# The order of scores and small products in three pipelined attentions of a decoder

## The chip, the cores and the metric

One NeuronCore of one Trainium2 chip. The metric is the device time of one execution of the whole kernel in microseconds, as the median of several runs. A profiled execution gives the trace.

## What is computed

Two decoder layers on x of shape (8, 128, 128), all in float32, with a plain layer norm over `x + block(x)` after each of six blocks. Three of the blocks are attentions with 16 heads of 8 channels. They are what the change touches:

```
x = norm(x + attn(x))                # attention 1: self attention, 128 queries, 128 keys
x = norm(x + cross(x, ctx))          # attention 2: 77 keys, q and k normalised per head
x = norm(x + mixture_top2(x))
x = norm(x + topk_attention_or_ssm(x))
x = norm(x + cross(x, ctx, mask))    # attention 5: 77 keys, masked
x = norm(x + experts(x))

scores = einsum('bhqd,bhkd->bhqk', q, k) * scale
p      = softmax(scores);  o = einsum('bhqk,bhkd->bqhd', p, v);  y = o @ Wo
```

## The kernel before

All three attentions are made by one set of helpers, one for each engine: `attention_tensor` (line 1406) on TensorE, `attention_scalar` (line 633), `attention_vector` (line 945) and `attention_pool` (line 500). Each walks over a step number i, with the 8 batches (B = 8) in a software pipeline, and each engine runs its instructions in the order in which they are written. Semaphores tie the engines together. The heads stand in G = 4 groups of J = 4.

In step i TensorE does, in this order:

- `shifted(i)` (from line 1426): scores of batch i, keys on the partitions, less the row maxima (lines 1443 and 1446; in the masked attention 5 also mask products, lines 1432 and 1438), into four banks, one for each group;
- `weigh(i-1)` (line 1462): probabilities times values;
- `flips(i)` (from line 1468): the output projection of batch i-3 (line 1473), the transpose of the maxima of batch i+1 (line 1477) and of the normalised output of batch i-2 (line 1480), into one bank;
- `scores(i+2)` (line 1422, with mask products at line 1418 in attention 5): scores of the batch two steps on, queries on the partitions, for the maxima alone;
- the transposes of outT of batch i-1 (line 1508).

ScalarE does exponentials (i,0) and (i,1) (line 641), copies outT of batch i-1 (line 652), copies the flipped bank (line 657), then does exponentials (i,2) and (i,3).

VectorE does the residual add of batch i-3 (line 974), which reads the flipped bank and waits for ScalarE's copy of it; the maximum of group 0 of batch i+2 (line 952); the reciprocal of batch i-1 (line 983), which waits for the outT transposes; the maximum of group 1; the normalisation into oN (line 995); the maxima of groups 2 and 3; a first remainder (line 962); the layer norm's apply for batch i-4 (line 1004), which waits for rstd from GpSimd; the second remainder; and the statistics of batch i-3 (lines 1010 to 1012). In attention 5 one more small instruction (line 987) follows the reciprocal. In attention 1 other small work stands behind steps 1, 2 and 3: the head sums for the keys of attention 2 and weight preparation.

GpSimd raises the variance to the power -1/2 for each batch (line 504). In attention 1 it first does three long powers (line 534) that need the head sums of VectorE's step 1, and two more between the batches.

PSUM has eight banks. Seven form a ring. The list `BURSTS` says in which order slots of the ring are given out: in each step four for the exponentials, one for the flips, four for the maxima. A slot waits for the reader of the slot seven places before it (`wait_bank`, line 149 on). For a slot of the flips the reader is ScalarE's copy and, from the third step on, VectorE's residual add.

Of the kernel before, what the change touches and what calls it, by code (L numbers as in the profile page):

```python
# [23 lines left out]
ALU = mybir.AluOpType  # L24
# [3 lines left out]
B, T, D = 8, 128, 128  # L28
# [71 lines left out]
RING_BANKS = [0, 1, 2, 3, 4, 5, 7]  # L100
BURSTS = [("max", 0), ("flip", -1), ("max", 1)]
for _i in range(B):
    BURSTS += [("exp", _i), ("flip", _i)] + ([("max", _i + 2)] if _i + 2 < B else [])
SLOTS = [(what, i, g) for what, i in BURSTS for g in range(1 if what == "flip" else G)]
PLACE = {slot: n for n, slot in enumerate(SLOTS)}

# [75 lines left out]
def _build(nc, ctx, a, out):  # L182
    def sb(name, shape, dt=F32):
        return ctx.enter_context(nc.sbuf_tensor(name, shape, dt))
# [4 lines left out]
    PS = ctx.enter_context(nc.psum_tensor("PS", [128, 8, 512], F32))  # L189
# [70 lines left out]
    R = sb("R", [128, B, D]); st = sb("st", [128, B, 6]); mv = sb("mv", [128, B, 2]); ve = sb("ve", [128, B]); rstd = sb("rstd", [128, B])  # L260
# [621 lines left out]
    def _(dve):  # L882
        V_ = nc.vector

        def step(ins):

            dve.wait_ge(dve_step.sem, dve_step.then(ins))
# [57 lines left out]
        def attention_vector(at, between):  # L945
            nk = at.nk

            def maximum(b, g):
                dve.wait_ge(at.scores_ready, G * b + g + 1)
                if b >= 3:  # L950
                    dve.wait_ge(at.flipped_ready, b - 2)
                V_.tensor_reduce(mxp[:, b % 3, g, 0:J],  # L952
                                 PS[:, at.bank("max", b, g), 0:J * nk].rearrange("p (j k) -> p j k", j=J),
                                 axis=AX.X, op=ALU.max).then_inc(at.max_ready, 1)

            def remainder(b, k):
                if k == 0:
                    dve.wait_ge(at.max_ready, G * (b + 1))
                else:
                    dve.wait_ge(at.part_ready, 2 * b + 1)  # L960
                whole = mxp[:, b % 3, :, J * k:J * (k + 1)]
                V_.tensor_tensor(mxp[:, b % 3, :, J * (k + 1):J * (k + 2)], whole, upper(mxp)[:, b % 3, :, J * k:J * (k + 1)],
                                 ALU.subtract).then_inc(at.part_ready, 1)

            for i in range(-2, B + 4):
                ahead, done, added, left = i + 2 < B, 0 <= i - 1 < B, 0 <= i - 3 < B, 0 <= i - 4 < B
                b, n, r = i - 4, i - 1, i - 3
                if added:
                    dve.wait_ge(at.proj_ready, r + 1)
                    if i < B + 2:  # L970
                        dve.wait_ge(at.flipped_copied, i + 2)
                    if r == 0 and not at.masked:
                        dve.wait_ge(at.xb_ready, 1)
                    V_.tensor_tensor(R[:, r, :], at.XB[:, r, :], PS[:, at.bank("flip", i), 2 * T:3 * T], ALU.add)\
                        .then_inc(at.residual_ready, 1)
                if ahead:
                    maximum(i + 2, 0)
                if done:
                    o = PS[:, at.out_bank(n), :].rearrange("p (h w) -> p h w", h=H)
                    dve.wait_ge(at.out_ready, n + 1)  # L980
                    if n >= 2:
                        dve.wait_ge(at.normed, n - 1)
                    ins = V_.reciprocal(rs[:, n % 2, :].rearrange("p (h o) -> p h o", o=1), o[:, :, HD:HD + 1])
                    if at.masked:

                        step(ins)
                        ins = V_.tensor_scalar(rs[:, n % 2, :], rs[:, n % 2, :], anykey[:], None, ALU.mult)
                    inverted = dve_step.then(ins)
                if ahead:
                    maximum(i + 2, 1)  # L990
                if done:
                    dve.wait_ge(dve_step.sem, inverted)
                    if n >= 2:
                        dve.wait_ge(at.flipped_ready, n + 2)
                    V_.tensor_tensor(oN[:, n % 2, :].rearrange("p (h d) -> p h d", h=H), o[:, :, 0:HD],
                                     rs[:, n % 2, :].rearrange("p (h o) -> p h o", o=1).to_broadcast([128, H, HD]),
                                     ALU.mult).then_inc(at.normed, 1)
                if ahead:
                    maximum(i + 2, 2)
                    maximum(i + 2, 3)  # L1000
                    remainder(i + 2, 0)
                if left:
                    dve.wait_ge(at.rstd_ready, b + 1)
                    V_.tensor_scalar(at.Xout[:, b, :], R[:, b, :], mv[:, b, 0:1], rstd[:, b:b + 1],
                                     ALU.subtract, ALU.mult).then_inc(at.x_ready, 1)
                if ahead:
                    remainder(i + 2, 1)
                if added:
                    dve.wait_ge(at.residual_ready, r + 1)
                    step(V_.bn_stats(st[:, r, :], R[:, r, :]))  # L1010
                    step(V_.bn_aggr(mv[:, r, :], st[:, r, :]))
                    V_.tensor_scalar(ve[:, r:r + 1], mv[:, r, 1:2], EPS, None, ALU.add).then_inc(at.eps_ready, 1)  # L1012
                if i in between:
                    between[i]()
# [22 lines left out]
        for c in range(2):  # L1037
            i = take(f"v1.{c}")
# [56 lines left out]
        i = take("logits8")  # L1095
# [60 lines left out]
        i = take("k5.1")  # L1156
# [12 lines left out]
        i = take("rank")  # L1169
# [3 lines left out]
        i = take("cumU")  # L1173
# [127 lines left out]
        for c in range(2):  # L1301
            i = take(f"dl.{c}")
# [11 lines left out]
        for e in range(E1 + 1):  # L1314
            if e < E1:
                for k in range(NI * 2):
                    n = e * NI * 2 + k
                    c, i = k // NI, k % NI
# [7 lines left out]
            if e == 0:  # L1326
                i = take("logits6")
# [28 lines left out]
    def _(pe):  # L1356
# [49 lines left out]
        def attention_tensor(at, between, idle, opening):  # L1406
# [5 lines left out]
            def scores(b):  # L1412

                for g in range(G):
                    at.wait_bank(pe, "max", b, g)
                if at.masked:
                    for g in range(G):
                        M_(PS[:, at.bank("max", b, g), 0:J * nk].rearrange("p (j k) -> p j k", j=J), identb[:],
                           maskneg[:].rearrange("p (o k) -> p o k", o=1).to_broadcast([128, J, nk]), start=True, stop=False)
                for g in range(G):  # L1420
                    dst = PS[:, at.bank("max", b, g), 0:J * nk].rearrange("p (j k) -> p j k", j=J)
                    M_(dst, qT[rows(g), b, :], at.kM[rows(g), :, b, :], start=not at.masked, stop=True)\  # L1422
                        .then_inc(at.scores_ready, 1)
# [27 lines left out]
            def weigh(b):  # L1451

                if b == 0:
                    aring.drain(pe)
                if b == B - 1:
                    at.wait_flip_read(pe, B - 2)
                elif b:
                    pe.wait_ge(at.normed, b)
                for g in range(G):
                    pe.wait_ge(at.exp_ready, G * b + g + 1)  # L1460
                    for j in range(J):
                        ins = M_(PS[32 * j:32 * j + 32, at.out_bank(b), 128 * g:128 * g + 128], at.V[0:nk, b, J * g + j, :],  # L1462
                                 PT[0:nk, b % 2, g, j, :], start=True, stop=True)
                ins.then_inc(at.pv_done, 1)
# [29 lines left out]
            for i in range(B + 4):  # L1494
                if i < B:
                    shifted(i)
                if i == 0:
                    opening[4]()
                if 0 <= i - 1 < B:
                    weigh(i - 1)  # L1500
                if i < B + 3:
                    flips(i)
                if i + 2 < B:
                    scores(i + 2)
                if 0 <= i - 1 < B:
                    pe.wait_ge(at.outT_copied, i)
                    for g in range(G):
                        ins = nc.tensor.transpose(PS[:, at.out_bank(i - 1), 128 * g:128 * g + 128], outT[:, g, :], ident[:])  # L1508
                    ins.then_inc(at.out_ready, 1)
                if i in between:  # L1510

                    pe.wait_ge(at.exp_ready, G * B)
                    between[i]()
# [158 lines left out]
        i = fill(dring, "scol")  # L1672
# [6 lines left out]
        i = fill(dring, "rank")  # L1679
# [5 lines left out]
        i = fill(dring, "cumU")  # L1685
# [53 lines left out]
        for e in range(2):  # L1739
            if e:  # L1740
                pe.wait_ge(event("sa_ready"), 1)
            for n in range(2):
                for c in range(4):
                    for a in range(2):
                        g = 2 * e + a
                        r = slice(32 * g, 32 * g + 32)
# [124 lines left out]
        for c in range(2):  # L1871
            i = fill(dring, f"dposA.{c}")
# [5 lines left out]
        for c in range(2):  # L1878
            if c:
                pe.wait_ge(event("chosen_copied"), 7 + NH)  # L1880
            i = fill(dring, f"dposS.{c}")
# [7 lines left out]
        for c in range(2):  # L1889
            dring.wait_copied(pe, f"dposS.{c}")  # L1890
            i = fill(dring, f"dl.{c}")
# [90 lines left out]
```

## Time and profile before

| | |
|---|---|
| median of 3 runs | 433.56 us (433.10 to 434.45) |
| the profiled execution | 434.33 us, of it span 432.5 us |
| TensorE matmul busy | 391.3 us (90%) |
| TensorE weight load busy | 262.1 us (61%) |
| VectorE busy | 280.9 us (65%) |
| ScalarE busy | 235.6 us (54%) |
| GpSimd busy | 130.5 us (30%) |
| attention 1, first to last shifted product | about 22.8 to 64 us |
| attention 2, the same | about 91.9 to 123 us |
| attention 5, the same | about 292 to 330 us |

Busy time overlaps between engines. The matmul's share is that of a pipelined engine, so 90% is not 90% of its peak. The chain of waits follows the work that ended last backwards; it names for each piece of time the engine that was waited for. The timeline gives the instructions in order of time.

### The profile page before, as it was taken

How to read it: one execution, taken by the hardware profiler on the slowest of the kernel's cores; microseconds unless marked ns; L12 is line 12 of the kernel's file. 1: busy time of each engine (PE TensorE's matmuls, PEld its weight loads, DVE VectorE, ACT ScalarE, POOL GpSimd, SP SyncE). 2: the span in 40 equal slices, each digit the busy share in tenths (PEclk: the TensorE clock that was granted, in tenths of full speed). 3: DMA queues.
4: the chain of work that ended last, by engine and by line, in shares of the span. 5: the costliest groups of instructions: out<-in, count | busy, mean ns of one | idle time of the engine just before them, and what ended most of it. 6: DMA issues, size and time to landing. Idle time of an engine off the chain costs nothing.

```text
span 432.5 us, 10063 instructions
## 1 busy us (share of the span) xinstructions
PE 391.3 (90%) x4041; PEld 262.1 (61%) x4050; DVE 280.9 (65%) x705; ACT 235.6 (54%) x441; POOL 130.5 (30%) x120
## 2 busy tenths in 40 slices
PE   5989798889999999977999999898999899999992
PEld 2556566546675946555676767645777466666662
DVE  6769656754765586897799897732566544444446
ACT  1855444736668267799999993025555442222220
POOL 6936952300113050004889893100011100000001
PEclk9999979999999999999999999989999999999998
DMA  6320000000000000020223220450000000000001
GB/s 176 74 49 2 4 2 2 1 2 3 3 5 0 2 0 2 6 109 23 90 89 102 93 81 2 131 163 2 3 4 4 2 0 0 2 0 1 2 0 48
DMA packets 16881, 13.84 MB, mean 32 GB/s; under 512 B 6548, under 2 KB 14133, under 8 KB 16837
## 3 DMA queue, kind: packets, MB, share of 16 engines
q1 hardware_dynamic: 15538, 12.51, 10.0%
q10 hardware_dynamic: 1299, 0.71, 0.5%
q8 instruction: 32, 0.52, 0.5%
q14 instruction: 12, 0.10, 0.1%
HBM read 12.64 MB, written 0.57 MB: 31 GB/s over the span
## 4 chain that ended last, share of the span: by engine, by line
PE 69%; ACT 11%; DVE 10%; POOL 5%; issue 4%; POOLq 0%; DVEq 0%; ACTq 0%
PE PS L1830 9%; PE PS L1909 6%; PE PS L1913 6%; PE PS L1940 6%; PE PS L1385 5%; PE PS L1443 5%; PE PS L1817 4%; POOL hr L534 4%; ACT att L641 3%; PE PS L1422 3%; PE PS L1371 2%; PE PS L1391 2%; PE PS L1508 2%; PE PS L1462 2%; ACT outT L652 2%
## 5 line engine op out<-in xcount | busy, mean ns | idle before, releaser
L641 ACT ACTIVATE att<-PS 77x512 f32<-77x512 f32 (+1 forms) x96 | 51.7, 591 | 47.2 <-PE PS L1446 47.2
L952 DVE TENSOR_REDUCE mxp<-PS 128x4 f32<-128x308 f32 (+1 forms) x96 | 48.0, 536 | 34.3 <-PE PS L1422 34.3
L878 ACT ACTIVATE kM<-PS 128x512 f32<-128x512 f32 x32 | 19.1, 597 | 55.5 <-PE PS L1909 54.4
L504 POOL TENSOR_TENSOR rstd<-ve,neg_half 128x1 f32<-128x1 f32 x24 | 13.1, 547 | 114.6 <-DVE ve L1012 114.6
L1258 DVE TENSOR_TENSOR_SCAN big<-big,PS 128x768 f32<-128x768 f32 x22 | 38.1, 1743 | 3.4 <-PE PS L1817 3.3
L1324 DVE TENSOR_TENSOR big<-kM,PS 128x512 f32<-128x512 f32 x32 | 21.9, 687 | 27.3 <-PE PS L1913 26.0
L498 POOL TENSOR_TENSOR rstd<-ve,neg_half 128x4 f32<-128x4 f32 x6 | 6.2, 1029 | 102.2 <-DVE ve L908 102.2
L1909 PE MATMUL PS<-xT,V 128*128 128x512 f32 x64 | 33.0, 597 | 1.1 <-DVE xT L1312 0.8
L1913 PE MATMUL PS<-xT,V 128*128 128x512 f32 x64 | 32.7, 592 | 0.0
L1940 PEld LDWEIGHTS PS<-big 128*128 128x128 f32 x256 | 29.7, 192 | 3.3 <-issue 3.3
L1371 PE MATMUL PS<-negsel,identb 128*128 128x512 bf16 x101 | 26.1, 400 | 6.1 <-DVE negsel L1024 4.4
L1940 PE MATMUL PS<-big 128*128 128x128 f32 x256 | 29.7, 275 | 0.0
L1446 PE MATMUL PS<-flipped,negsel 32*77 32x128 bf16 (+1 forms) x384 | 24.8, 219 | 0.0
L831 ACT ACTIVATE att<-big,BT 128x256 f32<-128x256 f32 x58 | 24.6, 497 | 0.0
L534 POOL TENSOR_TENSOR hr<-hvar,half_bh 77x32 f32<-77x32 f32 (+1 forms) x5 | 22.0, 4419 | 7.0 <-DVE hvar L935 7.0
L1345 DVE SCALAR_TENSOR_TENSOR R<-PS,aff,R 128x128 f32<-128x128 f32 x56 | 15.8, 345 | 11.2 <-PE PS L1940 11.2
L1443 PE MATMUL PS<-qT,kM 32*77 32x128 f32 x512 | 20.8, 276 | 1.8 <-ACT att L641 1.1
L1371 PEld LDWEIGHTS PS<-negsel,identb 128*128 128x128 bf16 x109 | 10.4, 102 | 19.1 <-issue 4.9
L1913 PEld LDWEIGHTS PS<-xT,V 128*128 128x128 f32 x64 | 12.2, 190 | 15.3 <-issue 14.8
L657 ACT ACTIVATE flipped<-PS 128x128 f32<-128x128 f32 (+1 forms) x33 | 10.7, 325 | 18.2 <-PE PS L1477 10.0
L1817 PE MATMUL PS<-ident,att 128*128 128x128 f32 x128 | 19.3, 273 | 1.2 <-ACT att L831 1.2
L1258 DVE TENSOR_TENSOR_SCAN untransposed<-untransposed,PS 128x768 f32<-128x768 f32 x10 | 17.5, 1748 | 4.4 <-PE PS L1817 4.1
(368 smaller groups left out, 894.6 us busy)
## 6 DMA issues: line engine op xcount, KB each, us to landing
kM<-Cdram SPq DMA_DIRECT2D x6, 384.0 KB, 3.5
XH<-Cdram SPq DMA_DIRECT2D x5, 384.0 KB, 3.3
xT<-Cdram SPq DMA_DIRECT2D x5, 384.0 KB, 3.4
V<-in_L_ffn_Wg SPq DMA_DIRECT2D x1, 1024.0 KB, 5.4
V<-in_L_ffn_Wu SPq DMA_DIRECT2D x1, 1024.0 KB, 8.0
out_x<-X SPq DMA_DIRECT2D x2, 256.0 KB, 2.3
ctxN<-in_ctx ACTq DMA_DIRECT2D x1, 308.0 KB
X<-in_x ACTq DMA_DIRECT2D x1, 256.0 KB, 4.0
```

The source lines that it names most:

```text
L534: P_.tensor_tensor(out=hr1[0:NC, n], in0=hvar[0:NC, n], in1=half_bh[0:NC, 0:n.stop - n.start], op=ALU.pow)\
L641: A_(PT[0:nk, i % 2, g], bank4(at.bank("exp", i, g), nk), ACT.Exp, scale=at.scale)\
L952: V_.tensor_reduce(mxp[:, b % 3, g, 0:J], PS[:, at.bank("max", b, g), 0:J * nk].rearrange("p (j k) -> p j k", j=J), axis=AX.X, op=ALU.max) ...
L1258: V_.tensor_tensor_scan(hst[m % NHS], dA[m % NDA], dBu[m % NDB], 0.0, ALU.mult, ALU.add)\
L1371: M_(PS[:, bank, :], identb[:], negsel[:].rearrange("p j t -> p (j t)"), start=True, stop=True)
L1443: M_(PS[0:nk, at.bank("exp", b, g), j * T:(j + 1) * T], at.kM[rows(g), j, b, :], qT[rows(g), b, :], start=not at.masked, stop=False)
L1446: ins = M_(PS[0:nk, at.bank("exp", b, g), j * T:(j + 1) * T], negsel[rows(g), j, 0:nk], upper(flipped)[rows(g), (b - 1) % 2, 0:T], start=F ...
L1817: ins = nc.tensor.transpose(dBu[n % NDB][:, 128 * k:128 * (k + 1)], scaled[s % 2][k][:, 128 * h:128 * (h + 1)], ident[:])
L1830: ins = M_(y_piece(h, lo, hi), ident[:], hC[n % NHC][:, lo:hi], start=False, stop=(n // NH == DS - 1 and (h, lo) != (0, 512)))
L1909: M_(PS[:, n % 2, :], Wg6[:, e, i * 128:(i + 1) * 128], half(xT, c), start=True, stop=True)\
L1913: M_(PS[:, 2 + n % 2, :], Wu6[:, e, i * 128:(i + 1) * 128], half(xT, c), start=True, stop=True)\
L1940: ins = M_(PS[:, 4 + (2 * e + c) % 4, b4 * D:(b4 + 1) * D], hidE[e % 2][:, i, b * T:(b + 1) * T], Wd6[:, NI * e + i, :], start=(i == 0), s ...
```

## The change

Three orders change, and no instruction is added or removed. In `BURSTS` the slots of the maxima of batch i+2 come ahead of the slot of the flips. On TensorE `scores(i+2)` is issued ahead of `flips(i)`. On VectorE the residual add moves from the head of the step to behind the normalisation, between the maxima of groups 1 and 2. ScalarE's and GpSimd's orders stay as they are.

```diff
 for _i in range(B):
-    BURSTS += [("exp", _i), ("flip", _i)] + ([("max", _i + 2)] if _i + 2 < B else [])
+    BURSTS += [("exp", _i)] + ([("max", _i + 2)] if _i + 2 < B else []) + [("flip", _i)]
@@ attention_vector
                 b, n, r = i - 4, i - 1, i - 3
-                if added:
-                    dve.wait_ge(at.proj_ready, r + 1)
-                    if i < B + 2:
-                        dve.wait_ge(at.flipped_copied, i + 2)
-                    if r == 0 and not at.masked:
-                        dve.wait_ge(at.xb_ready, 1)
-                    V_.tensor_tensor(R[:, r, :], at.XB[:, r, :], PS[:, at.bank("flip", i), 2 * T:3 * T], ALU.add)\
-                        .then_inc(at.residual_ready, 1)
                 if ahead:
                     maximum(i + 2, 0)
@@ behind the normalisation into oN
+                if added:
+                    dve.wait_ge(at.proj_ready, r + 1)
+                    if i < B + 2:
+                        dve.wait_ge(at.flipped_copied, i + 2)
+                    if r == 0 and not at.masked:
+                        dve.wait_ge(at.xb_ready, 1)
+                    V_.tensor_tensor(R[:, r, :], at.XB[:, r, :], PS[:, at.bank("flip", i), 2 * T:3 * T], ALU.add)\
+                        .then_inc(at.residual_ready, 1)
                 if ahead:
                     maximum(i + 2, 2)
                     maximum(i + 2, 3)
@@ attention_tensor
                 if 0 <= i - 1 < B:
                     weigh(i - 1)
+                if i + 2 < B:
+                    scores(i + 2)
                 if i < B + 3:
                     flips(i)
-                if i + 2 < B:
-                    scores(i + 2)
                 if 0 <= i - 1 < B:
                     pe.wait_ge(at.outT_copied, i)
```

## Rows read from the trace of the kernel before

**Rows 1.** The page, part 4: shares of the chain that ended last.

```profile
PE 69%; ACT 11%; DVE 10%; POOL 5%; issue 4%; POOLq 0%; DVEq 0%; ACTq 0%
```

**Rows 2.** Timeline, attention 2, step 4: start, us, engine, line, what; at last steps 5, 7.

```profile
113.76 0.46 PE L1443 MATMUL PS<-qT,kM 32*77 32x128 f32 x8 [0.16 <-ACT att L641]
...
115.21 1.07 ACT L641 ACTIVATE att<-PS 77x512 f32<-77x512 f32 x2 [1.55 <-PE PS L1446]
...
116.72 0.80 PE L1422 MATMUL PS<-kM,qT 32*128 32x308 f32 x8
...
117.10 1.07 ACT L641 ACTIVATE att<-PS 77x512 f32<-77x512 f32 x2
117.31 0.29 DVE L974 TENSOR_TENSOR R<-XB,PS 128x128 f32<-128x128 f32 x1 [0.96 <-ACT flipped L657]
...
117.45 0.66 PE L1508 MATMUL PS<-ident,outT 128*128 128x128 f32 x4
...
118.14 0.26 DVE L983 RECIPROCAL rs<-PS 128x16 f32<-128x16 f32 x1
...
118.27 0.46 PE L1443 MATMUL PS<-qT,kM 32*77 32x128 f32 x8 [0.16 <-ACT att L641]
118.32 0.42 DVE L952 TENSOR_REDUCE mxp<-PS 128x4 f32<-128x308 f32 x1
...
121.96 0.46 PE L1443 MATMUL PS<-qT,kM 32*77 32x128 f32 x8
```

**Rows 3.** Timeline, attention 2: exponentials of step 0, maximum 1 of step 1.

```profile
94.61 1.07 ACT L641 ACTIVATE att<-PS 77x512 f32<-77x512 f32 x2
...
96.08 0.46 PE L1443 MATMUL PS<-qT,kM 32*77 32x128 f32 x8 [0.72 <-DVE mxp L952]
...
100.29 0.41 DVE L952 TENSOR_REDUCE mxp<-PS 128x4 f32<-128x308 f32 x1
...
100.36 0.46 PE L1443 MATMUL PS<-qT,kM 32*77 32x128 f32 x8 [0.28 <-ACT att L641]
```

**Rows 4.** Timeline, attention 5: start of shifted and maximum 1, steps 2 and 6.

```profile
302.40 0.41 PE L1432 MATMUL PS<-first,maskrep 32*77 32x512 bf16 x4 [0.17 <-issue]
...
302.70 0.47 DVE L952 TENSOR_REDUCE mxp<-PS 128x4 f32<-128x308 f32 x1
...
323.87 0.41 PE L1432 MATMUL PS<-first,maskrep 32*77 32x512 bf16 x4 [0.16 <-issue]
...
324.18 0.47 DVE L952 TENSOR_REDUCE mxp<-PS 128x4 f32<-128x308 f32 x1
```

**Rows 5.** Timeline, attention 1: starts of steps 4 and 5, with the maxima between.

```profile
42.87 0.50 PE L1443 MATMUL PS<-qT,big 32*128 32x128 f32 x8 [0.37 <-DVE mxp L952]
...
47.17 0.69 DVE L952 TENSOR_REDUCE mxp<-PS 128x4 f32<-128x512 f32 x1
...
47.95 0.63 DVE L952 TENSOR_REDUCE mxp<-PS 128x4 f32<-128x512 f32 x1
...
48.11 0.50 PE L1443 MATMUL PS<-qT,big 32*128 32x128 f32 x8 [0.38 <-DVE mxp L952]
```

**Rows 6.** Timeline, attention 1: GpSimd's powers, and what comes behind them.

```profile
36.36 16.22 POOL L534 TENSOR_TENSOR hr<-hvar,half_bh 77x32 f32<-77x32 f32 x3 [7.04 <-DVE hvar L935]
...
53.13 0.35 DVE L1004 TENSOR_SCALAR X<-R,mv,rstd 128x128 f32<-128x128 f32 x1 [2.96 <-POOL rstd L504]
...
53.62 0.47 PE L1477 MATMUL PS<-ident,mxp 128*128 128x128 f32 x1 [2.52 <-DVE mxp L962]
...
54.23 2.09 PE L1422 MATMUL PS<-big,qT 32*128 32x512 f32 x8
...
62.45 0.50 PE L1443 MATMUL PS<-qT,big 32*128 32x128 f32 x8
```

**Rows 7.** Windows of attention 1: stretch, length, busy by engine, granted clock, DMA.

```profile
16.80:27.70 10.90, 9.18 (x91) 4.72 (x91) 8.07 (x15) 7.33 (x19) 7.23 (x9) 1.00 0.43 87
...
53.00:58.00 5.00, 4.38 (x26) 2.18 (x30) 2.54 (x9) 1.36 (x3) 5.00 (x4) 0.52 0.00 0
```

## Prediction

> **What bounds the kernel now.** I read the chain of waits first: TensorE has 69% of it, ScalarE 11%, VectorE 10% [rows 1]. The change touches only the three attentions, so I went to the timeline there, step by step. Call S the start of a step, the first product of shifted(i). In attention 2, TensorE runs shifted, weigh, flips, scores and the four outT transposes with hardly a gap: S is 113.76, the last transpose ends at 117.45+0.66 = 118.11, and the next S is 118.27 [rows 2]. Before that S TensorE stood still for only 0.16 us. ScalarE's second exponential pair ended at 117.10+1.07 = 118.17, so that pair and TensorE's own order bind almost together. In attention 5 the mask products make the step longer and TensorE binds alone: it stands for 0.16 us with the cause "issue" [rows 4]. In attention 1 the maximum of the first group binds: it ends at 47.17+0.69 = 47.86, the next S comes 0.25 us later at 48.11, and the row names VectorE's mxp as what ended the gap [rows 5]. So I take 0.25 us from the end of a maximum to the product that waits for it, and 0.10 us from the end of an exponential (118.17 to 118.27).
>
> Attention 1 also holds one large stall. GpSimd's three long powers (line 534) run from 36.36 to 52.58, and only behind them does it give rstd of the first batch. VectorE stands 2.96 us for it, until 53.13, at line 1004; the second remainder comes behind that, and flips(5) on TensorE waits 2.52 us until 53.62 [rows 6]. Through the stretch 53 to 58 the granted clock is 0.52, that is mostly the 1.2 GHz level, where 16.8 to 27.7 has 1.00 with TensorE busy for 9.18 of 10.90 us [rows 7].
>
> **The change part by part.** No instruction is added or removed. Three orders change.
>
> *TensorE.* scores(i+2) moves ahead of flips(i). The sum of the work is a permutation, so the outT transposes end at the same distance from S as now, 4.35 us in attention 2. flips(i) ends later by the length of the scores: 117.45-116.72 = 0.73 us in attention 2 [rows 2]. ScalarE's order is not changed: outT copy, flipped copy (line 657), then exponentials 2 and 3. The flipped copy waits for flips(i), and behind it in ScalarE's queue stand the two exponentials whose slots shifted(i+1) takes. So exp(i,3) ends 0.73 later, 118.90, and S could come at 119.00 instead of 118.27: +0.73.
>
> *Slots.* With nine slots a step and seven banks, shifted(i+1) now waits for exp(i,2), exp(i,3), flip(i) and max(i+2,0). After the change it is exp(i,2), exp(i,3), max(i+2,0) and max(i+2,1). That is a wait for one more maximum. On VectorE the reciprocal stands between maxima 0 and 1 and waits for the outT transposes, which stay last in TensorE's step. In the trace the reciprocal starts at 118.14, 0.03 after the last transpose, and maximum 1 runs from 118.32 to 118.74 [rows 2]. None of this moves in relation to S, so the next S can't be before 118.74+0.25 = 118.99: +0.72. The two ways give the same, and I take this one, since it gives every step from two rows: end of maximum 1, plus 0.25, less the next S. scores(i+3) in turn waits for maxima 2 and 3, for the read of flip(i) with its residual, and for exp(i+1,0). The last of these ends at about 115.21+0.54 = 115.75 (half of the pair's 1.07). The moved scores start a flips length before 116.72, so this is covered as long as the few products of flips take under 0.9 us, and they take some 0.6. flips(i) itself waits for exp(i,1), ended at 116.28, and now starts a flips length before 117.45: covered too.
>
> *VectorE.* The residual add (line 974) goes behind the normalisation, so maximum 0 no longer stands behind it. What waited for maximum 0 now waits for maximum 1 as well, so this buys nothing at the S. It delays maxima 2 and 3 by its own 0.29 us [rows 2]; they are wanted only at the next scores. I take zero, with that cover; without it 0.3 us a step.
>
> *Attention 2.* Five steps end in an S behind a scores. The first: 100.29+0.41+0.25-100.36 = 0.59; the last 0.72 [rows 2, 3]. The second is like the first (0.57), the third and fourth like the last (0.71, 0.72): together 3.3. Step 0 has no outT; there the exponential pair ends at 94.61+1.07, plus 0.73 and 0.10 gives 96.51 against S = 96.08: +0.4 [rows 3]. Sum **+3.7**, bounds 2.2 (each of the five shorter by the 0.25 of the hand-over, and step 0 by half) and 5.2 (each longer by the 0.3 of the residual add).
>
> *Attention 5.* The maximum is preceded by one more small instruction. First step: 302.70+0.47+0.25-302.40 = 1.02; last: 324.18+0.47+0.25-323.87 = 1.03 [rows 4]. The three between are 1.03, 1.04 and 0.93: together 5.05. Step 0 as in attention 2, +0.4. Sum **+5.5**, bounds by the same rule 4.0 and 7.0.
>
> *Attention 1.* Same rule: 47.95+0.63+0.25-48.11 = 0.72 a step [rows 5], four steps 2.9 with the others at 0.75, 0.71 and 0.72; step 0 is worth 0.3 by the exponential way. So S(5), now 48.11, comes at 51.3. GpSimd's powers start off VectorE's step 1, whose maxima move by some 0.2 us only, so rstd comes at about 53.3. By then maxima 2 and 3 and the first remainder of batch 6 have ended (about 52.9), VectorE waits 0.4 instead of 2.96, and the second remainder is there at 53.8, before flips(5) wants it: that now stands behind shifted, weigh and scores, which in attention 2 take 117.45-113.76 = 3.69 less the flips, so it comes at 54.1 or later. **The stall is filled by the slower steps and the clock has no long gap to fall in.** Step 5 is as long as step 4, 48.11-42.87 = 5.24 [rows 5], plus 0.72: S(6) = 57.3. Step 6 has no scores; attention 2 needs 121.96-118.27 = 3.69 for it [rows 2], and with the wider keys here I take 3.8: S(7) = 61.1 against 62.45 now [rows 6]. Sum **-1.4**, bounds -2.6 and +0.1 (five steps of the same 0.25 and 0.3). What is late next is maximum 1 in every step.
>
> Total -1.4+3.7+5.5 = **+7.8 us**. The profiled execution took 434.33 us (span 432.5); that would become 442.1. It lies 0.77 above the median of the runs shown, 433.56, so by the median **441.4 us**. Everything behind an attention only shifts: no transfer lands late there.
>
> **The clock, and the rule of the Trainium skill on it.** After the change TensorE stands about 0.9 us a step in attention 2 (119.00 less 118.11) and 1.2 in attention 5. The trace has a fall after a gap of 2.52 us [rows 6, 7] and none in a stretch that is 84% busy. The Trainium skill (TensorE: Matmul & The Clock Gate, The HAM clock gate) says that the clock follows how busy TensorE has recently been and that the unthrottled state has to be earned by activity. By that rule the added gaps could bring a fall of their own, which would add the price of the rival below; a step that stands 0.9 of 5.2 us is 83% busy, near to the stretch that kept its clock, so I forecast none.
>
> **The rivals.**
> 1. *The clock falls in the longer gaps.* The fall in attention 1 cost, from S(5) to S(7), 62.45-48.11 = 14.34 us against 5.24+3.8 = 9.0: 5.3, of which 2.5 are the stall and 2.8 the lower clock. One fall anywhere gives 444.2, one in each attention 449.8. Chance 0.12.
> 2. *The stall in attention 1 stays,* because the powers start later with the steps: then attention 1 costs +3.9 instead of -1.4: 446.7. Against it: VectorE's step 1 hardly moves. Chance 0.06.
> 3. *The slot wait bites only half.* If maximum 1 gets through earlier than its row shows, or the exponentials are released sooner, half of 9.2 in attentions 2 and 5 is left: about 437. Chance 0.14.
> 4. *Faster.* Place: flips(5) of attention 1. scores(7) now stands behind the 2.5 us stall and runs at the low clock, 2.09 us [rows 6]. Ahead of flips it runs while TensorE waits. If the steps did not get longer, this alone would give 433.56-2.0 = 431.5. It decides from a step price under 0.2 us (2.0 over ten steps of attentions 2 and 5). Against it: two independent ways both give 0.7 or more. Chance 0.07.
> 5. *The order does nothing,* since TensorE is full either way: 433.6. Chance 0.03.
>
> The forecast itself has 0.58. The range 437.0 to 446.0 takes in rival 3's value, the one fall of rival 1 and the bounds of the three sums (2.2+4.0-2.6 = 3.6 above the median gives 437.2, 5.2+7.0+0.1 = 12.3 gives 445.9). A measurement of this kernel can tell about 0.3% from no change. Slower by more than that 0.89, within 0.04, faster 0.07.
>
> **What would show it.** In the profile after: in attention 2, S to S of 5.2 instead of 4.5; in attention 5 of 6.4 to 6.5 instead of 5.4 to 5.5; a TensorE gap of about 1 us ahead of line 1443 or 1432 put down to VectorE's mxp or ScalarE's att; the reciprocal still right behind the transposes. In attention 1 steps of 5.9, VectorE's wait at line 1004 under 1 us, no granted clock under 0.9. The prediction is wrong if the exponentials 2 and 3 start before the flipped copy, if the reciprocal finds its transposes done earlier, or if the clock falls.

## The result, and the profile after

The changed kernel takes 440.53 us (median of 4 runs, 439.86 to 442.34) against 433.33 us before (431.92 to 434.45): a ratio of 1.017, 95% interval 1.013 to 1.022. That is slower by 7.2 us, clear of no change (the interval is +5.7 to +9.5 us); 441.4 was forecast, +7.8. All ratios below are to runs of the kernel before from the same round, and leave out the few that were over 1.5% slower than the fastest of their kernel.

The page of the changed kernel, parts 1 and 4 (busy time by engine, and the shares of the chain that ended last). GpSimd has gone from 5% to 1% of the chain, ScalarE from 11% to 12%, TensorE from 69% to 72% [rows 1]:

```profile
span 439.1 us, 10057 instructions
PE 385.6 (88%) x4041; PEld 260.4 (59%) x4050; DVE 281.1 (64%) x705; ACT 236.5 (54%) x441; POOL 130.6 (30%) x120
PE 72%; ACT 12%; DVE 10%; issue 4%; DMA 1%; POOL 1%; POOLq 0%; DVEq 0%; ACTq 0%
```

TensorE is busy for less time than before (385.6 against 391.3 us) in a longer span: the added time is gaps. The busy time itself is shorter because the granted clock was higher in the profiled execution, 0.990 on average against 0.980.

Timeline of the changed kernel, attention 2, one whole step from S = 110.14 to S = 115.39 (start, us, engine, line, what):

```profile
110.14 0.46 PE L1443 MATMUL PS<-qT,kM 32*77 32x128 f32 x8 [1.05 <-ACT att L641]
...
111.45 1.08 PE L1462 MATMUL PS<-att,V 77*32 77x128 f32 x32
112.46 0.80 PE L1422 MATMUL PS<-kM,qT 32*128 32x308 f32 x8
113.19 0.49 PE L1473 MATMUL PS<-Wp,flipped 128*128 128x128 f32 x2
...
113.74 0.60 PE L1508 MATMUL PS<-ident,outT 128*128 128x128 f32 x4
113.94 0.38 ACT L657 ACTIVATE flipped<-PS 128x256 f32<-128x256 f32 x1 [0.74 <-PE PS L1480]
114.22 1.07 ACT L641 ACTIVATE att<-PS 77x512 f32<-77x512 f32 x2
114.38 0.26 DVE L975 RECIPROCAL rs<-PS 128x16 f32<-128x16 f32 x1 [0.62 <-PE PS L1508]
114.55 0.42 DVE L952 TENSOR_REDUCE mxp<-PS 128x4 f32<-128x308 f32 x1
...
115.39 0.46 PE L1443 MATMUL PS<-qT,kM 32*77 32x128 f32 x8 [1.05 <-ACT att L641]
```

ScalarE now waits 0.74 us for the flips before it can copy them; before, the timeline shows no wait there. The exponentials behind the copy end at 115.29, and S comes 0.10 later. The reciprocal still starts right behind the transposes (114.34), and maximum 1 ends at 114.97. The gap of TensorE ahead of S is 1.05 us, where it was 0.16 [rows 2].

The span by stages, from the two timelines (S(0) is the first shifted product of an attention, S(7) the last batch's):

| stretch | before | after | change |
|---|---|---|---|
| start to S(0) of attention 1 | 22.86 | 23.22 | +0.36 |
| attention 1, S(0) to S(7) | 39.59 | 37.55 | -2.04 |
| to S(0) of attention 2 | 29.50 | 29.69 | +0.19 |
| attention 2, S(0) to S(7) | 30.01 | 33.86 | +3.85 |
| to S(0) of attention 5 | 170.13 | 169.08 | -1.05 |
| attention 5, S(0) to S(7) | 35.82 | 40.93 | +5.11 |
| the rest | 104.59 | 104.77 | +0.18 |
| span | 432.5 | 439.1 | +6.6 |

In attention 1, GpSimd's rstd still comes late, and VectorE still waits at line 1004, but for 1.19 us instead of 2.96, and TensorE no longer waits for what lies behind it. Timeline and windows of attention 1 after; the window answers to the second line of [rows 7]:

```profile
53.59 1.14 PE L1422 MATMUL PS<-big,qT 32*128 32x512 f32 x8
53.82 0.35 DVE L1004 TENSOR_SCALAR X<-R,mv,rstd 128x128 f32<-128x128 f32 x1 [1.19 <-POOL rstd L504]
54.08 0.17 DVE L962 TENSOR_TENSOR mxp<-mxp 128x16 f32<-128x16 f32 x1
...
54.98 0.27 PE L1477 MATMUL PS<-ident,mxp 128*128 128x128 f32 x1
...
60.77 0.50 PE L1443 MATMUL PS<-qT,big 32*128 32x128 f32 x8
```

```profile
53.00:58.00 5.00, 3.91 (x81) 2.74 (x73) 3.74 (x12) 2.68 (x6) 5.00 (x5) 1.00 0.01 3
```

The transpose of the maxima, which stood 2.52 us for the second remainder before [rows 6], runs at once, scores(7) take 1.14 us instead of 2.09, and the granted clock is 1.00 where it was 0.52.

### The profile page after: what moved, and what is told of

Same layout as the page of the kernel before. It is cut to its first block, busy times and chain, and to the rows that moved or that the text cites. A ratio compares the mean times of both kernels' runs of the same rounds, so it can differ in the third digit from the quotient of the medians.

```text
span 439.1 us, 10057 instructions
## 1 busy us (share of the span) xinstructions
PE 385.6 (88%) x4041; PEld 260.4 (59%) x4050; DVE 281.1 (64%) x705; ACT 236.5 (54%) x441; POOL 130.6 (30%) x120
## 4 chain that ended last, share of the span: by engine, by line
PE 72%; ACT 12%; DVE 10%; issue 4%; DMA 1%; POOL 1%; POOLq 0%; DVEq 0%; ACTq 0%
PE PS L1830 9%; PE PS L1443 6%; PE PS L1940 6%; PE PS L1909 6%; PE PS L1913 6%; PE PS L1385 5%; ACT att L641 5%; PE PS L1422 5%; PE PS L1462 4%; PE PS L1817 4%; PE PS L1371 3%; PE PS L1391 2%; PE PS L1642 2%; PE PS L1508 2%; PE PS L1380 1%
## 5 line engine op out<-in xcount | busy, mean ns | idle before, releaser
L1913 PEld LDWEIGHTS PS<-xT,V 128*128 128x128 f32 x64 | 12.2, 190 | 15.3 <-issue 14.8
L1443 PEld LDWEIGHTS PS<-qT,kM 32*77 32x77 f32 x512 | 15.9, 143 | 8.3 <-ACT att L641 7.7
```

The costliest lines, as they stand in the source:

```text
L1443: M_(PS[0:nk, at.bank("exp", b, g), j * T:(j + 1) * T], at.kM[rows(g), j, b, :], qT[rows(g), b, :], start=not at.masked, stop=False)
L1913: M_(PS[:, 2 + n % 2, :], Wu6[:, e, i * 128:(i + 1) * 128], half(xT, c), start=True, stop=True)\
```

## The experiments

**Theory:** two ways of nearly the same length make a step longer: ScalarE's queue (scores, flips, flipped copy, exponentials 2 and 3, S) and VectorE's (outT transposes, reciprocal, maximum 1, S). Each alone gives about 0.7 us a step. **Rivals:** only one of the two counts. The three parts of the change were tried alone on the old kernel, and the change was tried without its VectorE part; then each way was cut in the changed kernel. The step times below are from S to S in the profiled execution of each run. A step with a projection is one of the steps 3 to 5, in which flips also makes the output projection and VectorE does a residual add.

**The slots alone** (on the kernel before):

```diff
-    BURSTS += [("exp", _i), ("flip", _i)] + ([("max", _i + 2)] if _i + 2 < B else [])
+    BURSTS += [("exp", _i)] + ([("max", _i + 2)] if _i + 2 < B else []) + [("flip", _i)]
```

> The kernel before, with the new order of slots alone; TensorE and VectorE keep their old order. Theory (two ways of equal length, through VectorE's maximum 1 and through ScalarE's queue): shifted(i+1) now waits for maximum 1, which stands behind the reciprocal and the outT transposes, so the steps grow although TensorE's order is the old one: attention 2 step 4 to about 5.23 us (4.51 before), attention 5 to 6.4 (5.4 before), attention 1 to 5.96 (5.24), the cause of the gap named as VectorE's mxp; total about 441. Rival (ScalarE's queue alone makes the change slower, the slot wait is covered): steps stay 4.5 and 5.4, total 433.3.

Measured: 446.47 us, ratio 1.029 (1.022 to 1.036). The slot wait alone costs more than the whole change. Its timeline in attention 2:

```profile
113.08 0.46 PE L1443 MATMUL PS<-qT,kM 32*77 32x128 f32 x8 [0.88 <-DVE mxp L952]
...
115.66 0.49 PE L1473 MATMUL PS<-Wp,flipped 128*128 128x128 f32 x2 [0.19 <-ACT att L641]
...
117.89 0.41 DVE L952 TENSOR_REDUCE mxp<-PS 128x4 f32<-128x308 f32 x1
...
118.57 0.46 PE L1443 MATMUL PS<-qT,kM 32*77 32x128 f32 x8 [0.89 <-DVE mxp L952]
```

S is 0.27 after the end of maximum 1, as the theory has it, and the step is 5.49 us, not 5.23. The 0.26 more is the second row: with flips still ahead of scores on TensorE, the slot of flips(i) now waits for exponential (i,1). In the changed kernel scores stand there instead, and cover that wait: flips start at 113.19, 0.5 us after the exponential ended (111.59+1.08 = 112.67). The other attentions have the same addition (6.70 in attention 5, 6.22 in attention 1), which is why the total is 5 us above the 441 expected. The rival (steps stay) has fallen.

**TensorE's order alone** (on the kernel before, `scores(i + 2)` ahead of `flips(i)`, slots and VectorE as they were):

```diff
+                if i + 2 < B:
+                    scores(i + 2)
                 if i < B + 3:
                     flips(i)
-                if i + 2 < B:
-                    scores(i + 2)
```

> The kernel before, with scores ahead of flips on TensorE alone; slots and VectorE as before. Theory (two equal ways): the exponentials 2 and 3 stand behind the flipped copy, which now comes 0.7 us later: attention 2 step 4 about 5.2 us, attention 5 about 6.2 with a projection and 6.0 without, attention 1 about 5.9; total about 440.5. Rival (the slot wait alone makes the change slower): steps stay 4.5 and 5.4, total 433.3.

Measured: 446.83 us, ratio 1.031 (1.023 to 1.038); steps with a projection take 5.59 in attention 2 and 6.57 to 6.67 in attention 5. Timeline of its attention 2:

```profile
118.64 0.80 PE L1422 MATMUL PS<-kM,qT 32*128 32x308 f32 x8 [0.28 <-ACT att L641]
...
121.56 0.46 PE L1443 MATMUL PS<-qT,kM 32*77 32x128 f32 x8 [1.05 <-ACT att L641]
```

ScalarE's exponentials release S in attention 2, as expected (in steps 3 to 5 of attention 1 the rows name mxp). Again about 0.35 is on top, and again it is a slot that doesn't match: in the old order the last slot of scores waits for exponential (i,1), and the first row has that wait. Neither addition was expected; both totals came out 5 to 6 us above their expectation. So each half alone is dearer than the whole (+12.7 and +13.3 us, the ratio less one times 433.3, against +7.2 for the whole).

**VectorE's order alone** (on the kernel before, the residual add behind the normalisation as in the change, nothing else):

> The kernel before, with the residual add behind the normalisation on VectorE alone; slots and TensorE as before. In the old slot order shifted(i+1) waits for the read of flip(i), and from step 3 on that is the residual add, now behind the reciprocal and the normalisation. Theory (an order pays only with the slots that match it): in attention 2 steps 1 and 2 stay at 4.3 to 4.4 us, steps 3 to 5 grow from 4.51 to about 5.6 with VectorE's R as the cause; attention 5 steps 3 to 5 to about 6.7; in attention 1 about half of the stall is filled; total about 440. Rival (the place of this add costs nothing wherever it stands, as the prediction had it for the changed kernel): 433.3.

Measured: 441.01 us, ratio 1.018 (1.011 to 1.024). Steps 1 and 2 of attention 2 stay at 4.28 and 4.40, steps 3 to 5 are 5.72 (6.93 in attention 5), and the releaser is the residual add:

```profile
117.33 0.46 PE L1443 MATMUL PS<-qT,kM 32*77 32x128 f32 x8 [1.37 <-DVE R L996]
```

The part alone costs +7.6 us by the same rule, no more and no less than the whole within the intervals.

**The change without VectorE's part** (the residual add back at the head of the step):

> The changed kernel, with the residual add back at the head of VectorE's step; slots and TensorE as changed. Prediction's term: the move is worth nothing, since maximum 1 waits for the reciprocal anyway: steps stay at 5.23 (attention 2) and 6.39 (attention 5), total 440.5. Rival (with scores ahead of flips the add at the head makes maximum 0 wait for the flipped copy, and maximum 1 behind it): steps with a projection grow to about 5.75 in attention 2, 7.0 in attention 5 and 6.6 in attention 1, total about 446.

Measured: 448.81 us, ratio 1.035 (1.029 to 1.042). Here the prediction's term falls and the rival holds: steps with a projection are 5.70 (attention 2), 7.02 (attention 5) and 6.65 or more (attention 1), the others as in the changed kernel. Timeline of attention 2:

```profile
120.19 0.29 DVE L974 TENSOR_TENSOR R<-XB,PS 128x128 f32<-128x128 f32 x1 [2.54 <-ACT flipped L657]
120.39 0.47 DVE L952 TENSOR_REDUCE mxp<-PS 128x4 f32<-128x308 f32 x1
120.78 0.25 DVE L983 RECIPROCAL rs<-PS 128x16 f32<-128x16 f32 x1
120.94 0.41 DVE L952 TENSOR_REDUCE mxp<-PS 128x4 f32<-128x308 f32 x1
...
121.61 0.46 PE L1443 MATMUL PS<-qT,kM 32*77 32x128 f32 x8 [1.51 <-DVE mxp L952]
```

The add waits for the flipped copy, now late, and holds up maximum 0; the reciprocal starts 0.7 us after the transposes and no longer right behind them.

One step of attention 1 took 8.24 us, 1.5 more than the steps on both sides of it. TensorE had stood for 2.01 us before it, and the granted clock fell. Behind the next gap, of 1.96 us, it stayed at 1.00 (51 to 58), and behind the third, of 1.93, it fell again (0.60 from 60 to 64). In the same execution the gaps of 1.51 us a step in attention 2 and of 1.83 in attention 5 had a granted clock of 1.00. Window of attention 1:

```profile
48.00:52.00 4.00, 4.00 (x48) 2.55 (x40) 1.16 (x7) 1.64 (x4) 4.00 (x1) 0.68 0.01 2
```

So the rival of the prediction in which longer gaps bring the clock down did come true in this variant, though not in the changed kernel.

**ScalarE's way cut** (on the changed kernel, exponentials ahead of the flipped copy):

```diff
+                if 0 <= i < B:
+                    exponentials(i, (2, 3))
                 if i < B + 2:
                     ...
                     A_(flipped[:, i % 2, lo:hi], PS[:, at.bank("flip", i), lo:hi], ACT.Copy).then_inc(at.flipped_copied, 1)
-                if 0 <= i < B:
-                    exponentials(i, (2, 3))
```

> The changed kernel, with ScalarE's exponentials 2 and 3 ahead of its flipped copy. Theory (two equal ways): the way through maximum 1 is still there, so nothing is gained: attention 2 step 4 stays within 0.1 of 5.23 us, attention 5 within 0.1 of 6.39, and the cause named turns to VectorE's mxp; total 440.5 as the changed kernel. Rival (ScalarE's queue alone): step 4 falls to about 4.6, attention 5 to 5.4, total about 432.

Measured: 442.46 us, ratio 1.020 (1.011 to 1.028), no gain over the changed kernel. The step of attention 2 is 5.07, 0.16 shorter than 5.23 (0.1 was allowed), and the releaser turns, as expected:

```profile
109.41 0.46 PE L1443 MATMUL PS<-qT,kM 32*77 32x128 f32 x8 [0.88 <-DVE mxp L952]
...
114.49 0.46 PE L1443 MATMUL PS<-qT,kM 32*77 32x128 f32 x8 [0.88 <-DVE mxp L952]
```

So VectorE's way was 0.16 shorter than ScalarE's in attention 2. Step 0 fell by more, from 4.72 to 4.22: there is no reciprocal in it, and ScalarE's way stood alone. Steps with the full work stay at 6.39 in attention 5 and 5.80 in attention 1. From S(6) to S(7), where the flipped copy is wanted first, each attention loses 0.7 to 0.8 us (4.43 instead of 3.70 in attention 2). Together the three attentions take 0.4 us more than in the changed kernel (-0.49, +0.25 and +0.67 in attentions 2, 5 and 1).

**VectorE's way cut** (on the changed kernel, the reciprocal behind maximum 1):

```diff
                 if ahead:
                     maximum(i + 2, 0)
+                    maximum(i + 2, 1)
                 if done:
                     ...
-                if ahead:
-                    maximum(i + 2, 1)
```

> The changed kernel, with VectorE's reciprocal behind maximum 1 instead of ahead of it. Theory (two equal ways): the way through ScalarE's queue is still there: attention 2 step 4 stays at 5.23 us, attention 1 at 5.80, attention 5 loses only 0.15 a step (6.23 with a projection, 5.97 without), total about 439.8. Rival (the slot wait alone): step 4 falls to about 4.5, attention 5 to 5.4, total about 432.

Measured: 443.42 us, ratio 1.021 (1.014 to 1.028). Steps are 5.24 (attention 2), 5.77 (attention 1) and 6.23 with, 5.75 to 5.96 without a projection (attention 5), released by ScalarE but for one step. The three attentions are 1.1 us shorter than in the changed kernel, near the 0.7 expected, and yet the total is 2.9 us longer. In the profiled execution that lies outside of them: S(0) of attention 1 comes at 25.84 instead of 23.22, with no change in the code ahead of it, and the stretch ahead of attention 5 took 170.14 us instead of 169.08.

```profile
112.50 0.46 PE L1442 MATMUL PS<-qT,kM 32*77 32x128 f32 x8 [1.04 <-ACT att L641]
...
117.74 0.46 PE L1442 MATMUL PS<-qT,kM 32*77 32x128 f32 x8 [1.05 <-ACT att L641]
```

**Both ways cut** (both edits, the first in steps 0 to 5 only):

> The changed kernel with both ways cut at once: exponentials 2 and 3 ahead of the flipped copy on ScalarE in steps 0 to 5, and the reciprocal behind maximum 1 on VectorE. Theory (two ways of equal length, nothing else behind them): attention 2 step 4 falls from 5.23 to about 4.4 us, attention 5 to 5.35, attention 1 to 5.23, each at or below the kernel before; scores(7) of attention 1 runs ahead of GpSimd's stall. Total 430 to 432. Rival (the longer steps come from TensorE's new order itself, or from lower clock in its gaps): steps stay above 4.9 and 6.0, total 438 or more.

Measured: 432.58 us, the same as before (ratio 1.000, 0.997 to 1.004). The steps with a projection fall to 4.43 (attention 2) and 5.31 (attention 5), below the kernel before by about 0.08. Those of attention 1 take 5.2 to 5.3, above it in every step up to the fifth, by 1.0 us together, and steps 1 and 2 of the other two are up to 0.1 above it. Neither cut alone gave more than 0.17 in a step of attention 2 that has a reciprocal, both give 0.80 in steps 3 to 5: that shows two parallel ways. What comes next behind them is short: the flipped copy itself, for which the products of the next step wait too, and TensorE's own order.

```profile
116.91 0.26 DVE L978 RECIPROCAL rs<-PS 128x16 f32<-128x16 f32 x1 [0.23 <-PE PS L1509]
117.12 0.46 PE L1444 MATMUL PS<-qT,kM 32*77 32x128 f32 x8 [0.24 <-ACT flipped L659]
```

The next products start 0.21 us after the reciprocal has started, no longer behind it and a maximum. With short steps the stall of attention 1 is back: VectorE waits 2.40 us at the layer norm's apply, and the granted clock is 0.50 from 57 to 60.

**One long power of GpSimd moved behind the first rstd.** On the kernel before, on the changed one, and on the version with both cuts:

```diff
-        for _ in range(3):
+        for _ in range(2):
             key_rstds()
-        steps = iter([key_rstds, key_rstds])
+        steps = iter([key_rstds, key_rstds, key_rstds])
```

> The kernel before, with one of GpSimd's three long powers of attention 1 moved behind the first rstd (two ahead, three between the batches). Theory (the stall behind the powers and the clock fall after it cost the kernel before 5.3 us): VectorE's wait at the layer norm's apply goes, no clock of 0.5 near 54, S(7) of attention 1 comes at about 57.2 instead of 62.45, total about 428.5. Rival (a later wait on GpSimd takes its place, since the powers have to be done anyway): S(7) at 60 or later, total above 431.

> The changed kernel with the same move of one power behind the first rstd. Theory (in the changed kernel the slower steps already fill the stall, so the stall is no longer on TensorE's path): S(7) of attention 1 stays within 0.3 us of 60.77, the total stays at that of the changed kernel, and against the kernel before with the same move the changed one is 12 us slower. Rival (the stall still costs the changed kernel something): S(7) before 60, total below 439.

> The changed kernel with exponentials ahead of the flipped copy, reciprocal behind maximum 1, and the power moved. Theory: steps of 4.4 (attention 2), 5.35 (attention 5) and 5.2 (attention 1), no stall and no low clock in attention 1: about 427.5, at or a little below the kernel before with the power moved. Rival (the two cuts give nothing over the old order): equal to the kernel before with the power moved, or slower.

Each ratio is to the kernel before in the same round; its median there was 433.54 for the second row and 433.56 for the last two.

| kernel | median | ratio to before | attention 1, S(0) to S(7), profiled execution |
|---|---|---|---|
| before | 433.33 us | | 39.59 |
| before, power moved | 428.77 us | 0.989 (0.984 to 0.994) | 34.35 |
| changed | 440.53 us | 1.017 (1.013 to 1.022) | 37.55 |
| changed, power moved | 440.10 us | 1.015 (1.010 to 1.019) | 37.55 |
| both ways cut, power moved | 428.81 us | 0.989 (0.985 to 0.994) | 35.33 |

Timeline of the kernel before with the power moved: rstd comes at 50.00, ahead of the third power, and flips runs without a wait.

```profile
49.45 0.55 POOL L504 TENSOR_TENSOR rstd<-ve,neg_half 128x1 f32<-128x1 f32 x1
49.96 5.44 POOL L534 TENSOR_TENSOR hr<-hvar,half_bh 77x32 f32<-77x32 f32 x1
52.38 0.34 DVE L1004 TENSOR_SCALAR X<-R,mv,rstd 128x128 f32<-128x128 f32 x1
...
53.22 0.27 PE L1477 MATMUL PS<-ident,mxp 128*128 128x128 f32 x1
```

The move is worth 5.24 us of attention 1 in the kernel before (5.3 was the prediction's price for stall and clock) and nothing in the changed one, 37.55 both times. So the slower steps had filled the stall there. S(7) came at 59.51 on the span's clock and not at the 57.2 expected, since S(0) was late, at 25.16; from S(0) on the expectation holds (34.35 against 57.2-22.86 = 34.3). Against the kernel before with the power moved, the change costs 11.3 us, and that is its price where no stall takes part of it back. Both cuts with the power moved are as fast as the old order with the power moved (428.81 and 428.77 us), so the two cuts give nothing over the old order. By the three attentions the old order is 0.8 us shorter (100.1 against 100.9).

Not all of this gain is there in every execution. Of 13 runs of the kernel before in one round, two had a mean granted clock of 0.992 and took 429.67 and 429.84 us, three had 0.988 and took 431.2 to 431.5, and eight had 0.979 to 0.984 and took 433.0 to 434.7. With the power moved the four runs were 427.4 and 428.1 at 0.992 and 429.4 and 429.5 at 0.988. At equal mean clock the move is thus worth about 2 us, by few runs; the rest of the 4.6 by the medians came with the clock.

## Why the prediction was right

**Direction and size.** +7.2 us measured by the medians, +7.8 forecast. The stage table has +3.85, +5.11 and -2.04 for attentions 2, 5 and 1, forecast +3.7, +5.5, -1.4. Their sum is +6.9, 0.9 less than forecast.

**Two ways of equal length.** This held, and is shown by the two cuts and their sum. In attention 2 the longer is ScalarE's by 0.16. In attention 5 it is VectorE's in every step behind the first: cutting it shortens steps 1 and 2 from 6.01 and 6.12 to 5.75 and 5.96, and steps 3 and 4 from 6.38 and 6.39 to 6.23, and cutting ScalarE's shortens none of them. In steps 3 to 5 the row names ScalarE's att all the same, since the exponential ended 0.01 us after the maximum (323.65 and 323.64, S at 323.90), but in this trace a product comes 0.25 us after a maximum where that is last and 0.10 after an exponential. In steps 3 to 5 of attention 1 the two are within 0.03 us. Step 0, which has ScalarE's way alone, grew by 0.59 in attention 2 instead of 0.4; the part above 0.4 stays open.

**The size of a step.** Attention 2: 5.23 to 5.25, forecast 5.23. Attention 5: 6.01 to 6.39, forecast 6.2 to 6.4; its five steps grew by 4.67 instead of 5.05. Attention 1: 5.80, forecast 5.96; up to S(5) it grew by 2.6 us, forecast 3.2. The step of the prediction that was off is "a permutation, so the outT transposes end at the same distance from S". They end earlier: 49.40+0.60-45.29 = 4.71 in attention 1 against 42.50-37.63 = 4.87, and 4.20 against 4.35 in attention 2. In VectorE's way through maximum 1 that is the whole difference to the formula, in attention 1 directly, and in attention 2 with ScalarE's way cut (5.07 against 5.23). Weight loads of TensorE, attention 2, the kernel before:

```profile
116.72 0.31 PEld L1422 LDWEIGHTS PS<-kM,qT 32*128 32x128 f32 x8 [0.17 <-issue]
117.45 0.42 PEld L1508 LDWEIGHTS PS<-ident,outT 128*128 128x128 f32 x4 [0.42 <-issue]
```

And of the changed kernel:

```profile
113.19 0.30 PEld L1473 LDWEIGHTS PS<-Wp,flipped 128*128 128x128 f32 x2 [0.42 <-issue]
113.63 0.47 PEld L1508 LDWEIGHTS PS<-ident,outT 128*128 128x128 f32 x4
```

Before, TensorE goes from full products to products on 32 rows (flips to scores) with a gap of 0.17 us, and back (scores to outT) with one of 0.42. Neither waits for another engine: the copy of outT had ended at 116.82. After, the gap of 0.42 stands behind scores as before, now ahead of flips, and flips and outT follow each other as full products without a gap; the 0.17 is gone. The Trainium skill (TensorEngine Tiling (Array Packing), Key Properties) says that changing the tiling mode drains TensorE; the two traces agree, with 0.15 to 0.16 us for one switch fewer. It is a comparison of traces and no experiment of its own. Attention 5 speaks for it: there a full mask product (line 1418) stands between flips and scores in both kernels, no switch goes, and steps 3 to 5 came only 0.03 to 0.05 us short of the formula. Its steps 1 and 2 were 0.16 and 0.11 short, which this does not explain.

**VectorE's move.** The term zero was right for the sum and wrong in its reason. The prediction said that taking the add away from maximum 0 "buys nothing at the S". Without the move, steps with a projection are longer by 0.47 us in attention 2, by 0.63 in attention 5 and by 0.85 or more in attention 1. The formula for a step, maximum 1 at its present distance from S, held only because the add had left the head: with the flipped copy late, the add would have held up everything on VectorE. That this term came out at zero was luck: the two effects, a late copy and an add out of its way, cancel, and the prediction named neither.

**The stall.** GpSimd's powers started at 36.96 instead of 36.36; 0.36 of this is the later S(0), so the step moved them by 0.24, forecast 0.2. VectorE waited 1.19 us at line 1004, forecast 0.4 and "under 1 us". The steps up to S(5) had grown by 2.6 and not 3.2, so counted from S(0) VectorE was there 0.6 earlier, and rstd 0.1 later, than forecast. TensorE did not notice, flips(5) came later still. S(7) came at 60.77, forecast 61.1, with no low clock. From S(5) to S(7) attention 1 takes 9.68 us instead of 14.34; 9.8 was forecast. How much this gives back depends on the execution that it is compared with: the mean granted clock of the kernel before went from 0.979 to 0.992 from run to run, and its profiled one had 0.980. Which stretches were spared at 0.992 isn't recorded.

**Luck in the comparison of the two profiles.** The stretch ahead of attention 5 was 1.05 us shorter after, and the code of that stretch is the same but for the last steps of attention 2. Windows of the kernel before, then of the changed one, in which the same instructions come 2.9 us later:

```profile
280.00:285.00 5.00, 4.31 (x12) 1.87 (x13) 1.12 (x4) 1.79 (x3) 0.02 (x1) 0.69 1.09 341
```

```profile
280.00:285.00 5.00, 2.95 (x17) 1.60 (x15) 3.85 (x18) 0.70 (x2) 1.85 (x2) 1.00 1.02 342
284.00:288.00 4.00, 3.77 (x17) 1.87 (x17) 0.08 (x1) 1.97 (x4) 0.00 (x0) 1.00 1.08 331
```

Before, the clock fell there, behind gaps of 1.37 and 0.69 us; after, with the same instructions and gaps of 1.37 and 0.68 us, it did not. From the first of these gaps to the mask products of attention 5 it took 10.40 us before and 8.80 after. Without the whole 1.05 the spans would differ by 7.7 us instead of 6.6; the 7.2 of the medians lies between.

**The rivals.** Clock falls in the longer gaps: none in the attentions of the changed kernel (granted clock 1.00 in all three), although TensorE stood 0.94 to 1.39 us ahead of every S behind a scores; with gaps of about 2 us, in the change without VectorE's part, it did fall. The stall stays: fell. The slot wait bites half: fell, by the slots alone. Faster by scores(7) ahead of the stall: with both ways cut S(5) to S(7) of attention 1 takes 12.06 us instead of 14.34, near the 2.0 that the rival gives it, though the clock still fell. The first five steps of attention 1 lost 1.0 of that again, and the total was that of the kernel before.

## What to carry to other kernels

When an item is moved in an in-order queue, look at who copies its neighbour out and what is queued behind that copy on the other engine: here 0.73 us on TensorE came back in full through ScalarE. A ring's slot order, the issue order and the readers' order are one design; each part alone cost 7.6 to 13.3 us, the three together 7.2, and two of them without VectorE's 15.3. And before pricing a change to a pipeline, look for a stall downstream that it may fill: it hid 4 of 11 us here, and removing it was worth 4.6 us by the medians, more than the 2.0 that the prediction's rival gave the change at best.

## What the runs showed of the hardware that was not expected

- Whether the clock falls behind gaps of 1.37 and 0.69 us differs from one profiled execution to the next, with the same instructions there. From 278 to 292 us, ahead of attention 5, the granted clock is 0.88 in four of the twelve traces (the kernel before, ScalarE's way cut, VectorE's way cut, both ways cut with the power moved) and 1.00 in eight. The stretch from S(7) of attention 2 to S(0) of attention 5 takes 168.3 us in six of these eight, 169.1 in the changed kernel and with the slots alone, 170.1 to 170.2 in three of the four and 171.1 in the last. The longest and the shortest differ by 0.6% of the kernel.
- The time to the first shifted product was 22.7 to 23.2 us in eight traces and 25.1 to 25.8 in four, between kernels that are the same up to there. In two of the four (VectorE's order alone, the old order with the power moved) the granted clock is 0.72 from 10 to 16 us; the other two show 1.00 there, and the cause stays open.
- Gaps of 1.51 to 1.83 us in every step left the granted clock at 1.00 in attentions 2 and 5 of the change without VectorE's part; of three gaps in its attention 1, of 2.01, 1.96 and 1.93 us, it fell behind the first and the third.
- One switch between full and 32-row products less went with 0.15 to 0.16 us a step less in attentions 1 and 2.
